# An attention and FFN kernel: the identity products ahead of the first FFN tile wait for the row sums

## The reference

```python
x = L0_attn_x                                        # (4, 1024, 512)
x = x + _layernorm(_L0_attn_ref(_layernorm(x), ...)) # windowed attention of 16-channel tokens, two branches
x = x + _layernorm(_L0_ffn_ref(_layernorm(x), ...))

# _L0_ffn_ref, hidden 512, inner 2048, int8 weights:
gate = silu(einsum(x, w_gate) * s_gate)
up   = einsum(x, w_up) * s_up
return einsum(gate * up, w_down) * s_down
```

## Time and profile before

| | us |
|---|---|
| median of 3 runs | 1006.89 |
| lowest, highest | 1006.85, 1008.29 |
| profiled execution, its own time | 1008.13 |
| its span, first to last instruction | 1006.4 |
| TensorE busy | 908.8 |
| VectorE busy | 838.3 |
| GpSimd busy | 726.6 |
| ScalarE busy | 626.4 |

### The profile page before, as it was taken

The page is one execution under the profiler, slowest core; times in us unless marked ns, Lnnn a source line. Parts: engine busy times, 40 slices in busy tenths (PEclk is TensorE's granted clock), DMA queues, the critical chain, the costliest instruction groups (busy, mean ns, idle before and its releaser), DMA issues. The chain is left out here.

```text
span 1006.4 us, 18403 instructions
## 1 busy us (share of the span) xinstructions
PE 908.8 (90%) x6503; PEld 708.1 (70%) x6503; DVE 838.3 (83%) x1201; ACT 626.4 (62%) x1058; POOL 726.6 (72%) x582
## 2 busy tenths in 40 slices
PE   3626628999999999999999999999999999999996
PEld 3424418777777777877777777777787777777773
DVE  6898898899899999999999989999999989353122
ACT  2745825867586767766686758676776665452431
POOL 3556656798879886998789877988699888552333
PEclk9866968999999999999999999999999999999999
DMA  6011050014102320114002410232011302220001
GB/s 179 0 43 42 1 125 1 1 42 110 39 2 64 85 64 0 28 51 116 13 1 62 99 47 0 63 83 63 1 28 53 76 14 64 55 52 1 22 2 42
DMA packets 78320, 46.14 MB, mean 46 GB/s; under 512 B 39609, under 2 KB 72377, under 8 KB 78265
## 3 DMA queue, kind: packets, MB, share of 16 engines
q1 hardware_dynamic: 73400, 45.10, 17.1%
q10 hardware_dynamic: 4864, 0.32, 0.3%
HBM read 28.63 MB, written 16.78 MB: 45 GB/s over the span
## 5 line engine op out<-in xcount | busy, mean ns | idle before, releaser
L1134 DVE TENSOR_TENSOR prod<-ps_x,qkvl 128x2048 f32<-128x2048 f32 x128 | 290.8, 2281 | 10.6 <-ACT ps_x L789 6.7
L653 PE MATMUL ps_gate<-xhi,wg 128*128 128x256 f16 x1024 | 230.5, 273 | 2.3 <-DVE xlo L1253 1.7
L653 PE MATMUL ps_up<-xhi,wu 128*128 128x256 f16 x1024 | 230.5, 273 | 0.0
L653 PE MATMUL ps_up<-xlo,wu 128*128 128x256 f16 x1024 | 230.5, 273 | 0.0
L653 PE MATMUL ps_gate<-xlo,wg 128*128 128x256 f16 x1024 | 230.5, 273 | 0.0
L859 ACT ACTIVATE gact<-ps_gate,sgate 128x256 f32<-128x256 f32 x256 | 106.9, 468 | 158.8 <-PE ps_gate L653 157.2
L1028 POOL TENSOR_TENSOR flo<-fuse,fhi 128x512 f16<-128x512 f32 x128 | 148.8, 1163 | 77.6 <-ACT fhi L865 77.6
L968 POOL TENSOR_TENSOR sum<-prod 128x1024 f32<-128x1024 f32 x64 | 150.6, 2363 | 40.3 <-DVE prod L1134 37.5
L1262 DVE SCALAR_TENSOR_TENSOR fuse<-ps_up,sup,gact 128x256 f32<-128x256 f32 x256 | 110.1, 471 | 82.6 <-PE ps_up L653 70.7
L977 POOL TENSOR_TENSOR sum<-prod 128x1024 f32<-128x1024 f32 x64 | 151.6, 2371 | 19.5 <-DVE prod L1134 12.9
L673 PE MATMUL ps_acc<-wd,fhi 128*128 128x512 f16 x512 | 153.3, 379 | 0.0
(11 more groups left out here) (152 smaller groups left out, 1401.6 us busy)
## 6 DMA issues: line engine op xcount, KB each, us to landing
xb<-in_L_attn_x SPq DMA_DIRECT2D x64, 128.0 KB, 2.7
xr<-in_L_attn_x SPq DMA_DIRECT2D x16, 512.0 KB
attn_rows<-ratt SPq DMA_DIRECT2D x16, 512.0 KB, 3.5
o<-attn_rows SPq DMA_DIRECT2D x32, 256.0 KB, 4.2
out_x<-y SPq DMA_DIRECT2D x15, 512.0 KB
x<-in_L_ffn_w_gate SPq DMA_DIRECT2D x1, 1024.0 KB, 5.3
xr<-in_L_ffn_w_up SPq DMA_DIRECT2D x1, 1024.0 KB, 8.4
out_x<-y SPq DMA_DIRECT2D x2, 256.0 KB
```

Source lines behind the costliest of these rows:

```text
L653: mm = nc.tensor.matmul(ps[:, HALF * i:HALF * i + HALF], w[:, k, P * j:P * j + P], xs[:, k, rows], start=(k == 0 and part == 0), stop=(k = ...
L1134: nc.vector.tensor_tensor(prod[:, half].rearrange("p (s j k) -> p s j k", j=WIN, k=WIN), left[:, :, None, :].broadcast_to([P, 4 * WIN, WIN ...
```

## The change

One wait of TensorE has another semaphore: that of the four row sums in `xr` in place of that of the statistics over them.

```diff
             def warm_fx(t, bank):
-                pe.wait_ge(f_stats, 2)
+                pe.wait_ge(xr_sum, NQ)
                 warm(0, 8, bank)
```

## The result

| | kernel before | changed kernel |
|---|---|---|
| median of 20 runs each | 1007.63 us | 1005.74 us |
| lowest, highest | 1006.55, 1008.74 | 1004.91, 1007.42 |
| profiled execution, its own time | 1008.13 | 1005.57 |

The ratio is 0.9984, with a 95% interval of 0.9978 to 0.9990: 1.0 to 2.2 us of 1007.6 us. That is just under the 0.2% which the prediction set as the bound of "the same". The three runs that stood ahead of the prediction were a low sample of the kernel before: their median was 1006.89 us, that of twenty is 1007.63 us.

A forecast was written before the change was run, and what follows sets the result against it. TensorE bounds the kernel from the first gate product on; that product comes 1.61 us sooner, 1008.13 to 1006.52 us. Against the median 0.37 us is left; forecast 1006.7 us, range 1005.3 to 1008.5 us.

The forecast's parts named there:

- The removed wait: TensorE's 16 identity products ahead of the transposes start with the last row sum, at 149.70 us, 2.97 us sooner.
- What is late next: ScalarE's scaling and copy L789 hold the first xhi copy to about 158.05 us, capping the gain at 1.61 us.
- the sum: Profiled execution of 1008.13 us less 1.61 us by which the first gate product comes sooner: 1006.52 us.
- Behind it: After the first gate product, GpSimd's idle 5.92 us covers the 1.61 us; three later TensorE waits move along with ScalarE.
- rival 1: TensorE's clock falls in the new 2.3 us gap behind the transposes, giving 1.5 us back: 1008.2 us; chance 0.35.
- the 1.24 us: Distance of the earlier median, 1006.89 us, below the profiled execution; attributed to runs whose clock happens to rise soon.
- usual run: Typical execution of the changed kernel, forecast at 1006.7 us (1006.3 to 1007.0 us), chance 0.50.
- the stated range: Forecast range for the changed kernel's time, from rival 3 to the upper end of rival 1: 1005.3 to 1008.5 us.
- rival 3: Every run loses the 1.61 us, the profile-to-median distance having nothing to do with the block: 1005.3 us; chance 0.09.
- Rival 2: Clock falls and a second stretch stays low through holes behind slower gate products, price 3.4 us: 1010.0 us; chance 0.06.

The follow-up runs named there:

- qx_behind: Changed kernel with ScalarE's copy L789 placed behind its two xhi copies; median 1005.85 us, ratio 0.9982 to the kernel before.
- before_again: The kernel before, unchanged, profiled a second time in one run; 1008.02 us.
- after_third: The changed kernel, nothing altered, run and profiled a third time; median 1005.76 us, its profiled execution 1007.42 us.
- old_wait_8: Kernel with the old wait (statistics) but 8 identity products in place of 16; median 1006.46 us, ratio 0.9989 to the kernel before.
- new_wait_8: Changed kernel (new wait) with 8 identity products in place of 16; median 1008.65 us, ratio 1.0015 to the kernel before.
- early_clock: Changed kernel plus 8 identity products, four behind the pair product and four behind the scale row, at some 14 and 17 us; median 1006.57 us.

## Why the prediction was right, and which step was not

- **The removed wait.** Products 2.56 us after the first row sum: measured 2.56 (148.91 - 146.35). Their length was taken as 6.35 us with the rise after 5.65; it was 6.17 us. The choice did not matter, as said, because ScalarE came last.
- **What is late next.** Forecast from the first row sum: transposes 8.96, xhi copy 10.91, gate product 12.98 us. Measured: 9.04, 10.82 and 12.87 us. The copy stood behind L789 without a wait, and qx_behind moved the gate product by moving L789. Term of the sum: 1.61 us forecast, 1.72 and (against before_again) 1.71 us measured.
- **Behind it** nothing was given back in two of the three profiles: 844.6 against 844.7 us. The third is rival 1, below.
- **The step that failed** is the one from the profile to the median, "If the 1.24 us are this, 1.61 - 1.24 = 0.37 us is left against the median". It took most of the gain for something that a usual run had already, and the three runs for typical. They were low by 0.7 us; the median moved by 1.9 us (1.0 to 2.2 us by the interval), and the lowest run by 1.46 us. In both profiles of before the products ran into the transposes in the same way. So the "usual run" of 1006.7 us was too high: it is 1005.74 us, outside the 1006.3 to 1007.0 us that had the chance of 0.50. It lies inside the stated range because of rival 3 (the whole gain shows on the median, 1005.3 us, chance 0.09), which came closest; its size of 1.61 us lies inside the measured interval. That the range held is owed to its width, and not to the forecast.
- **The profiled execution** took 1005.57 us, 0.95 us less than the 1006.52 us of the sum. 0.11 us of that is the block, 0.79 us the earlier first row sum, which has nothing to do with the change.
- **A slip in the working**: rival 1 starts from 1006.65 us, a number that stands nowhere else; the sum gives 1006.52 us and the forecast 1006.7 us. Nothing hangs on it.
- **Rival 1** was given 1.5 us and a chance of 0.35. It is real: 1.7 us in one of three profiled executions of the changed kernel. As a share of all executions it is not shown; the mean clocks suggest 5 in 42. It does not undo the gain at the median.
- **Rival 2** did not come: TensorE stays busy behind the first gate product, and one low stretch is all that any of these profiles of unchanged length shows there.
- That the Trainium skill ("TensorE: Matmul & The Clock Gate", part 1) calls the monitor free-running is borne out by after_third, where the clock rose at 152.8 us, 3.8 us after the first product, against some 153.8 us and 4.9 us in the other two profiles of the same program. The conclusion that I drew from it, a smaller gain at the median, is not.

## What to carry to other kernels

Products that only keep TensorE's clock up are part of the schedule. In this kernel they did best when they ended just before the work that they precede was ready (sixteen, 3 us earlier, 0.3 us of idle time behind them); when they ended 2.9 us too late that cost 1.7 us, and when idle time of 2.7 us or more followed them, the clock fell or had not risen, and the first eight of them alone at the new place cost 1 us against the old state.

Before explaining the distance between a profiled execution and a median, look at how far the runs of one kernel spread. Here three runs spread over 1.4 us and twenty over 2.2 us, and the median of the three was 0.7 us low; lining the traces up at an instruction ahead of the change gave the effect to 0.1 us.

## What was not expected of the hardware

Taking 16 products, 64 instructions of TensorE with their weight loads, out of a prologue made the loop behind it slower by 24 us, with six idle times of 2.15 to 2.86 us, the clock down beside them, and 59 in place of 33 instruction packets; taking out 8 (old_wait_8, new_wait_8) or moving the 16 did not. A program's length is a variable of an experiment that removes instructions.

TensorE's clock also stayed low in early_clock although the engine was busy for 11.06 us of 11.1 us ahead of the rise at 25.8 us. The clock column reads 1.00 ahead of the first record of a trace; that the level was the lower one is read from the transposes at 19.57 us (1.11 us in place of 0.60). Later in the same trace the clock rose some 5 us into a busy stretch.
